# A graph network kernel: rankings, placing and unit records laid inside the counting of edges, and node layers handed from chunk to chunk

## The reference

```python
# stage 1: three graph-convolution layers 16 -> 64 -> 64 -> 16
deg = segment_sum(ones, col, N)              # with one loop per node added
norm = deg**-0.5 [row] * deg**-0.5 [col]
def gcn_layer(h, W, b):
    h = h @ W
    return segment_sum(norm[:, None] * h[row], col, N) + b
h = relu(gcn_layer(x, W1, b1)); h = relu(gcn_layer(h, W2, b2)); h = gcn_layer(h, W3, b3)
x = layernorm(x + h)
# stage 2: edge-conditioned attention, 16x16 channels per edge
w_m, w_a = edge_attr @ W_msg + b_msg, edge_attr @ W_attn + b_attn     # (E, 16, 16) each
e1, e2 = w_m * x[src][:, :, None], w_a * x[src][:, :, None]
attn = segment_softmax(e2, dst)
x = layernorm(x + segment_sum(e1 * attn, dst, N).sum(axis=1))
```

## Time and profile before

| what | us |
|---|---|
| median of three executions | 2631.48 (2610.61 to 2644.78) |
| span of the profiled execution, first to last instruction | 2618.5 |
| the median less the span | 13.0 |
| DVE busy | 1989.2 (76%) |
| PE busy | 1880.0 (72%) |
| ACT busy | 1458.7 (56%) |
| POOL busy | 1289.6 (49%) |

### The profile page before, as it was taken

The page is one execution under the profiler, slowest core; times in us unless marked ns, Lnnn a source line. Parts: engine busy times, 40 slices in busy tenths (PEclk is TensorE's granted clock), DMA queues, the critical chain, the costliest instruction groups (busy, mean ns, idle before and its releaser), DMA issues.

```text
span 2618.5 us, 37987 instructions
## 1 busy us (share of the span) xinstructions
PE 1880.0 (72%) x5814; PEld 706.3 (27%) x5815; DVE 1989.2 (76%) x3269; ACT 1458.7 (56%) x4999; POOL 1289.6 (49%) x1520
## 2 busy tenths in 40 slices
PE   2445676577982577787887777877888877888855
PEld 1111111132341133233333333333333333333322
DVE  5678999752011588888888888888898898988866
ACT  5124444210001576676777767777776776776643
POOL 2200000425556566656666657666666665666650
PEclk9789989788975699999999989999998998998877
DMA  2000000000001000000000000000000000000000
GB/s 31 17 23 4 0 0 0 2 10 17 11 13 15 9 10 10 9 10 9 10 9 10 9 10 9 10 9 10 9 10 9 10 10 9 9 10 9 9 5 7
DMA packets 85243, 25.74 MB, mean 10 GB/s; under 512 B 61677, under 2 KB 82271, under 8 KB 85087
## 3 DMA queue, kind: packets, MB, share of 16 engines
q0 software_dynamic: 36672, 18.09, 5.7%
q1 hardware_dynamic: 48463, 6.91, 1.8%
q10 hardware_dynamic: 80, 0.43, 0.1%
HBM read 22.73 MB, written 2.51 MB: 10 GB/s over the span
## 4 chain that ended last, share of the span: by engine, by line
issue 29%; DVE 25%; PE 23%; DVEq 17%; ACT 3%; POOL 1%; another core or an unknown queue 1%; DMA 1%; ACTq 0%; POOLq 0%; PEldq 0%; PEld 0%
PE pair L820 9%; DVE eo L1471 6%; DVE hot L1197 4%; DVEq L1490 4%; PE pw L711 3%; DVE eo L1514 2%; DVE eo L1505 2%; PE pw L807 2%; PE pw L708 2%; PE pw L707 2%; DVE top L1486 2%; ACT eo L1021 2%; DVE top L1491 2%; DVE bank L1499 2%; DVEq L1503 1%
## 5 line engine op out<-in xcount | busy, mean ns | idle before, releaser
L626 POOL DMA_INDIRECT nbr<-table,rec x928 | 961.0, 1036 | 527.3 <-ACT eo L1021 274.0
L820 PE MATMUL pair<-eo,ident 128*128 128x512 f32 x1856 | 890.0, 625 | 12.4 <-issue 7.7
L1021 ACT ACTIVATE eo<-pw,nbr 128x32 f32<-128x32 f32 x3712 | 694.3, 371 | 83.1 <-issue 66.9
L1471 DVE TENSOR_TENSOR eo<-pw,nbr 128x1024 f32 (+1 forms) x348 | 412.5, 1218 | 169.3 <-PE pw L807 94.4
L820 PEld LDWEIGHTS pair<-eo,ident 128*128 128x128 f32 x1856 | 366.2, 201 | 494.9 <-issue 479.6
L807 PE MATMUL pw<-wk,termsT 100*128 100x512 bf16 x928 | 307.5, 417 | 249.8 <-issue 173.8
L1197 DVE TENSOR_SCALAR hot<-iota_key,near_key 128x500 bf16<-128x500 f16 x974 | 273.8, 346 | 59.3 <-issue 31.9
L1010 ACT ACTIVATE eo<-eo 128x2048 f32<-128x2048 f32 x116 | 221.5, 1910 | 107.4 <-DVE eo L1505 85.1
L1514 DVE TENSOR_TENSOR eo<-eo x232 | 272.7, 1216 | 5.9 <-issue 4.0
L1505 DVE TENSOR_TENSOR eo<-eo,bank (+1 forms) x116 | 265.3, 2287 | 10.7
L672 PE MATMUL bank<-hot 128*128 128x500 bf16 x488 | 146.7, 414 | 145.4 <-DVE hot L1197 93.1
(11 more groups left out here) (245 smaller groups left out, 1815.6 us busy)
## 6 DMA issues: line engine op xcount, KB each, us to landing
nbr<-table,rec POOLq DMA_INDIRECT x928
rec<-unit_recs SPq DMA_DIRECT2D x116, 8.0 KB
attr<-in_edge_attr_dram,rec POOLq DMA_INDIRECT x116
unit_recs<-place SPq DMA_DIRECT2D x27, 64.0 KB
shared<-key_row SPq DMA_DIRECT2D x1, 1600.0 KB, 6.7
counts<-in_dst_dram SPq DMA_DIRECT2D x1, 448.0 KB
counts<-in_src_dram SPq DMA_DIRECT2D x1, 448.0 KB
place<-in_src_dram,at_i POOLq DMA_INDIRECT x26, 2.6
```

The costliest lines, as they stand in the source:

```text
L626: pool.indirect_dma_start(nbr[:, b, j * FEAT:(j + 1) * FEAT], None, table, bass.IndirectOffsetOnAxis(ap=rec[:, b, j:j + 1], axis=0)).then_ ...
L820: mm = pe.matmul(total, ident[:], eo[:, ring, j * 2 * CH:(j + 1) * 2 * CH], start=False, stop=(j == SLOT - 1), skip_group_check=True)
L1021: done = act.activation(eo[:, ring, lo:lo + wide], pw[:, j - 4, c * wide:(c + 1) * wide], ACT.Copy, scale=nbr[:, held, j * FEAT + c:j * FE ...
L1471: dve.tensor_tensor(eo[:, bass.ds(ring, 1), k * 4 * CH:(k + 1) * 4 * CH] .rearrange("p r (c f) -> p (r c) f", f=2 * FEAT), pw[:, 2 * (k % ...
```

## The change

- **Gathers** are issued two per pair of windows: POOL waits for DVE's window counter `s_near`, and for the gather four before, with four semaphores in place of one.
- **Counting below** is spread over pairs 5 to 17 on ACT, two tiles after each pair.
- **Ranks** begin four pairs later, at pair 22, one tile a pair; each tile is ranked in two halves of 1600 keys, one after each window. POOL adds the halves, makes the place and writes each tile's record at once.
- **Placing** (`place_nodes`, now only the copies) moves to DVE's pair 56 and the unit arithmetic (`unit_counts`) to pair 59, both within the counting.
- **The square roots** are written and laid over `y2T` by ACT's queue and no longer by SP's.
- **Layers:** with one plane PE no longer waits for `s_parts` in layers 1 and 2. It waits inside chunk 0 for each four tiles that DVE has split (`s_split`). The product with b2 stands behind `s_parts`. `plane_tables` is run in layers 1 and 2 only for several planes.

```diff
...
             for t in range(NT + 1):
                 to = dst_blk[:, t, :] if t < NT else dst_blk_last
+                if t % 2 == 0:
+                    pool.wait_ge(s_near, t + 5)
+                if t >= 4:
+                    pool.wait_ge(s_dblk[t % 4], 16 * (t // 4))
                 pool.indirect_dma_start(to, None, dst_blocks,
...
-            pool.wait_ge(s_rank, 1)
-            pool.tensor_scalar(rank_f, rank_f, NP - 1.0, 0.5, ALU.add, ALU.mult)
-            pool.drain()
-            pool.tensor_copy(rank_i, rank_f)
-            pool.drain()
             for t in range(NT):
+                here = slice(t, t + 1)
+                pool.wait_ge(s_rank, t + 1)
+                pool.tensor_tensor(rank_f[:, here], rank_f[:, here], rank_h[:, here], ALU.add)
+                pool.drain()
+                pool.tensor_scalar(rank_f[:, here], rank_f[:, here], NP - 1.0, 0.5, ALU.add, ALU.mult)
+                pool.drain()
+                pool.tensor_copy(rank_i[:, here], rank_f[:, here])
+                pool.drain()
                 pool.indirect_dma_start(rec_place, bass.IndirectOffsetOnAxis(ap=rank_i[:, t:t + 1], axis=0),
                                         rec_s[:, t, :], None).then_inc(s_recd, 16)
...
                 for a in range(NG):
+                    if layer and c == 0 and a % CT == 0:
+                        pe.wait_ge(s_split, splits + a // CT + 1)
+                        pe.sem_inc(s_settled_pe, 1)
                     cols = counts[:, a * DPAD + lo:a * DPAD + lo + n]
...
+            def count_below(t):
+
+                block_t = dst_blk[:, t, :] if t < NT else dst_blk_last
+                act.wait_ge(s_dblk[t % 4], 16 * (t // 4 + 1))
+                act.activation(signs[:, 0:P], block_t, ACT.Sign, bias=node_m[:, t:t + 1],
+                               scale=-1.0, accum_out=below[:, t:t + 1])
+                act.drain()
+
+            def rank_half(t, v):
+
+                part = slice(v * (NP // 2), (v + 1) * (NP // 2))
+                act.activation(signs[:, part], key_all[:, part], ACT.Sign, bias=key_neg[:, bass.ds(t, 1)],
+                               accum_out=(rank_f, rank_h)[v][:, bass.ds(t, 1)])
+                done = act.drain()
+                if v == 1:
+                    done.then_inc(s_rank, 1)
...
+            below_from = 5
+            rank_from = below_from + NT // 2 + 1 + 4
...
+                        keep_counts(0, below_from)
+                        for k in range(0, NT + 1, 2):
+                            keep_counts(below_from + k // 2, below_from + k // 2 + 1)
+                            with act.If(c < 1):
+                                for t in range(k, min(k + 2, NT + 1)):
+                                    count_below(t)
+                                if k + 2 > NT:
+                                    act.drain().then_inc(s_below, 1)
+                        keep_counts(below_from + NT // 2 + 1, rank_from)
                         with act.Fori(0, NT) as t:
...
+                            w = act.snap(wins, min_val=0, max_val=MANY)
+                            for v in range(2):
+                                keep_window(t + rank_from, w, v)
+                                with act.If(c < 1):
+                                    act.wait_ge(s_keyb, 16)
+                                    rank_half(t, v)
+                            act.reg_add(wins, wins, 1)
+                        keep_counts(rank_from + NT, NWIN // 2)
...
+            place_at = 56
...
-                    plane_tables()
                     if layer == 0:
-                        one_hot_plane()
+                        plane_tables()
+                        one_hot_head()
+                        one_hot_pairs(0, place_at)
                         with dve.If(c < 1):
-
-                            dve.wait_ge(s_rank, 1)
+                            place_nodes()
+                        one_hot_pairs(place_at, place_at + 3)
+                        with dve.If(c < 1):
+                            unit_counts()
+                        one_hot_pairs(place_at + 3, NWIN // 2)
+                        with dve.If(c < 1):
+
+                            dve.wait_ge(s_rank, NT)
...
                     dve.drain().then_inc(s_parts, 1)
-                    if layer == 0:
-                        with dve.If(c < 1):
-                            place_nodes()
+                    if layer == 1:
+                        with dve.If(p < 1):
+                            dve.wait_ge(s_sdb, 16)
+                            dve.wait_ge(s_sdc, 16)
+                            dve.tensor_scalar(y2T, y2T, b2c[:], None, ALU.mult)
+                            dve.drain()
...
```

More of the change, by code:

```diff
@@ L258, in gnn_kernel @@
         s_winr = sem("s_winr")
-        s_dblk = sem("s_dblk")
+        s_dblk = [sem(f"s_dblk{v}") for v in range(4)]
         s_below = sem("s_below")
@@ L422, in _ @@
             sp.dma_start(rec_p[:], rec_place.rearrange("(t p) c -> p t c", p=P)).then_inc(s_recp, 16)
[L424 to L428, removed]
             job = sp.alloc_register("sp_jobs")
@@ L696, in count_plane, with gather_chunk @@
                     pe.reg_add(wins, wins, 1)
-            def gather_chunk(layer, c, base):
+            def gather_chunk(layer, c, base, splits):
                 v = c % 2
@@ L746, in sum_sources @@
                 base = (c * ((NCH + 1) // 2), c * (NCH // 2))
+                splits = c * NCH if layer else None
                 for k in range(NCH + (2 if layer == 1 else 1)):
                     if k < NCH:
-                        gather_chunk(layer, k, base)
+                        gather_chunk(layer, k, base, splits)
                     if 1 <= k <= NCH:
@@ L764, in _, with counted @@
                     c = pe.snap(plane, min_val=0, max_val=MANY)
-                    pe.wait_ge(s_planes, c + 1)
-                    pe.sem_inc(s_settled_pe, 1)
+                    def counted():
+                        pe.wait_ge(s_planes, c + 1)
+                        pe.sem_inc(s_settled_pe, 1)
+                        count_plane()
+                        pe.wait_ge(s_parts, c + 1)
+                        pe.sem_inc(s_settled_pe, 1)
                     if layer == 0:
-                        count_plane()
+                        counted()
                     else:
                         with pe.If(np_ > 1):
-                            count_plane()
-                    pe.wait_ge(s_parts, c + 1)
-                    pe.sem_inc(s_settled_pe, 1)
+                            counted()
                     sum_sources(layer, c, pe.snap(mid, min_val=0, max_val=MANY))
@@ L892, in _, with keep_window @@
                 act.reg_mov(r, 0)
+            def keep_window(i, w, v):
+                act.wait_ge(s_full[v], w + 1)
+                act.copy(counts[:, 0:NG * DPAD].rearrange("p (a d) -> p a d", a=NG)
+                         [:, :, bass.ds(i * 2 * WIN + v * WIN, WIN)],
+                         bank[v][:, 0:NG * WIN].rearrange("p (a d) -> p a d", a=NG)
+                         ).then_inc(s_full_free[v], 1)
             def keep_counts(lo, hi):
@@ L898, in keep_counts @@
                     for v in range(2):
-                        act.wait_ge(s_full[v], w + 1)
-                        act.copy(counts[:, 0:NG * DPAD].rearrange("p (a d) -> p a d", a=NG)
-                                 [:, :, bass.ds(i * 2 * WIN + v * WIN, WIN)],
-                                 bank[v][:, 0:NG * WIN].rearrange("p (a d) -> p a d", a=NG)
-                                 ).then_inc(s_full_free[v], 1)
+                        keep_window(i, w, v)
                     act.reg_add(wins, wins, 1)
@@ L937, in _ @@
                 if layer == 1:
+                    act.wait_ge(s_sdd, 16)
+                    act.dma_start(y2T[:, 0:Y2A], row(sd_row[0:Y2A]).broadcast_to([HID, Y2A])).then_inc(s_sdb, 16)
                     act.wait_ge(s_y1, 1)
-                    act.wait_ge(s_sdd, 16)
                     act.dma_start(y2T[:, Y2A:NG * P], row(sd_row[Y2A:NG * P]).broadcast_to([HID, NG * P - Y2A])
@@ L1204, in one_hot_plane, with one_hot_pairs @@
                 dve.drain()
-                with dve.Fori(0, NWIN // 2) as i:
+            def one_hot_pairs(lo_pair, hi_pair):
+                with dve.Fori(lo_pair, hi_pair) as i:
                     w = dve.snap(windows, min_val=0, max_val=MANY)
@@ L1311, in place_nodes, with unit_counts @@
                 dve.drain().then_inc(s_place, 1)
+            def unit_counts():
                 dve.wait_ge(s_dmax, 1)
```

42 lines of the change are left out of this document (19 added, 23 removed).

## The result

| what | before | after |
|---|---|---|
| median of four executions, us | 2628.47 (2610.61 to 2644.78) | 2541.11 (2538.57 to 2550.02) |
| ratio, 95% interval | | 0.9686 [0.9636, 0.9736] |
| span of the profiled execution, us | 2618.5 | 2538.0 |

The spans differ by 80.5 us and the medians by 87.4, since the medians stand 10.0 and 3.1 us above the profiled spans. Little of that is time around a span: the profiled execution of the changed kernel took 2539.8 us, 1.8 above its own span, and every execution on record with both figures has between 1.7 and 2.8. What follows is about the 80.5. That difference is part of the finding. The chip of the first measurement is not on record.

The account below looks back on a forecast made before the run. DVE was taken to pace the counting, with only the 811 us before attention able to shrink. Gains 86.7 less costs 10.6 gave net 76.1: span 2542.4, plus 13.0, 2555 us; range of 8 in 10: 2536 to 2597.

Parts of the forecast that it names:

- the 13.0 us that I took as lying around the span: Whole execution: 13.0 us added to the forecast span of 2542.4 to give the forecast time of 2555.
- gathers: Counting, first burst: two gathers per pair of windows avoid DVE's slow windows; gain 22.5 us, bounds 0 to 24.9.
- keys: Counting: spread below-counts and four pairs before ranking cover the wait for keys; gain 22.3 us, bounds 15 to 22.3.
- ranks and price of places: Counting: ACT's half ranks pace part of 50 windows, cost 2 us; spread place writes still cost 1.8.
- placing and unit arithmetic: Counting: this work, formerly hidden behind PE's first chunk, now counts in full on DVE; cost 5.6 us, bounds 4 to 13.
- burst of places gone, rounds beside DVE: Late counting: 14.9 us excess of the place-write burst goes; unit-record rounds beside DVE's last 20 pairs cost 3.
- seams: PE's idle time ahead of layers 1 and 2, 19.0 and 6.45 us, goes; gain 25.5, bounds 18 to 28.
- start of attention: Before attention: early unit records let the table go out sooner; gain 3.3 us, bounds 1 to 4.
- the halting: Counting: DVE's own sequencer runs slow beside back-to-back indirect DMAs; excess 24.9 and 14.9 us in two bursts.
- my bound for new code to be fetched: Placing and unit arithmetic on DVE: cost up to 13 us if entering new code costs a fetch.
- Rival B: Counting: POOL's operations hold up DVE in full, 54 and 17 us; time 2623, no change; chance 0.12.
- rival A: Counting: DVE's slow sequencer is not cured by spreading; gains fall by 35.6 us, time 2591; chance 0.14.

Follow-up runs that it names:

- second chip: Kernel before and changed kernel, both unchanged, measured again later on another chip: changed kernel 2352.98 us, ratio 0.9816 to the kernel before.
- the run with one pair: Changed kernel with ACT's rankings starting one pair after the last below-count instead of four: 2361.76 us, ratio 0.9845 to the kernel before.
- the run with late records: Changed kernel with placing and unit arithmetic back behind the counting, in layer 0: 2373.97 us, ratio 0.9892 to the kernel before.
- The two runs above: Changed kernel with rankings one pair after the last below-count (2361.76 us), or with below-counts in a row and the four-pair gap kept (2365.43 us).

## Why the prediction was right

The time, 2541.1, lies in the range and 14 us below the 2555 forecast. The span was forecast at 2542.4 and is 2538.0, 4.4 us of the miss. The other 10 come from the 13.0 us that I took as lying around the span. No run shows that term: every execution on record with both figures has 1.7 to 2.8 us. I had set the median of three executions against the span of another, and these executions range over 34 us. In the terms of the forecast, from starts of windows and the rows above:

| term | forecast | first measurement | second chip |
|---|---|---|---|
| gathers: windows 1 to 41 | +22.5 | 133.6 - 110.3 = +23.3 | 116.7 - 110.2 = +6.5 |
| keys: 41 to 51 | +22.3 | 49.4 - 30.4 = +19.0 | 50.3 - 26.6 = +23.7 |
| ranks and price of places: 51 to 111 | -3.8 | 166.1 - 165.7 = +0.4 | 164.6 - 165.7 = -1.1 |
| placing and unit arithmetic: 111 to 121 | -5.6 | 28.4 - 33.1 = -4.7 | 29.5 - 33.1 = -3.6 |
| burst of places gone, rounds beside DVE: 121 to 159 | +11.9 | 118.1 - 108.7 = +9.4 | 106.6 - 108.8 = -2.2 |
| seams | +25.5 | 244.4 - 218.6 = +25.7 | 245.0 - 218.6 = +26.4 |
| start of attention | +3.3 | 16.4 - 12.8 = +3.6 | 14.2 - 12.7 = +1.4 |
| rest: head, end of counting, attention | 0 | 0.6 - 0.5 + 3.7 = +3.8 | 0.9 + 0.0 - 3.5 = -2.6 |
| sum | 76.1 | 80.5 | 48.6 |

(The second chip's sum is taken from unrounded terms.) The 6.5 us of the gathers on the second chip are not the halting: the granted clock of the kernel before was 0.82 from 44.7 to 90.4 us and 0.74 from 90.4 to 181 there, and spreading the gathers alone brought nothing. A term read from one pair of traces carries that much chance: windows 1 to 41, with the gathers spread, took 110.1 to 110.3 us in seven traces and 115.8 and 117.9 in two, where the granted clock was 0.85.

- *Keys.* 3.3 us under the forecast, and not for its reason: the stretch meets the dip of the clock at 158 to 180 us. On the second chip, with the clock at 0.92 there, the same ten windows give 23.7. My step, that the keys come some 14.5 us after the last below-count and four pairs cover it, is shown by the run with one pair.
- *Ranks.* ACT at 2.74 us a window was to pace 50 windows in part. The first thirty were 0.05 us longer each (2.80 against 2.75), the rest not; over the stretch nothing was lost. Within the bounds.
- *Placing and arithmetic.* 4.7, near the 5.6; my bound for new code to be fetched wasn't needed.
- *Rounds beside DVE.* I took 3 us; the run with late records puts it between 0.6 and 4.1. I had the rounds' pace wrong: 12.3 us each (380.5 to 491.4, nine rounds), not 9.4. POOL was held, not DVE. The multiplication L580 takes 382 ns in the median after 500 us, beside DVE's windows 566, and over 1 us in four of nine:

```profile
L580 POOL TENSOR_SCALAR place<-place x9: 452/566/1373, 390.0 to 483.2; 128x64 f32<-128x64 f32 x9
```

```profile
L580 POOL TENSOR_SCALAR place<-place x14: 382/382/1487, 512.5 to 634.1; 128x64 f32<-128x64 f32 x14
```

All of POOL's operations together take 0.52 us each from 382 to 491 us (65.03 us for 125) and 0.35 from 503 to 640 (68.96 for 196). DVE's hot rows keep their median of 344 ns both there and at 183 to 350 us. The page of the Trainium skill that the prediction weighed ("SBUF — State Buffer", Who interferes with whom) says whoever comes second blocks; the rows agree in that an operation is longer on one side, POOL's, beside a DVE busy 96% of the time. Which came first no row shows, and the price on DVE stayed at 4 us or less. Rival B needed DVE to be the loser, and falls. The slower rounds cost nothing, since the records were 72 us early.
- *Seams and the start of attention* came out within 0.3 us of their terms. POOL's last round begins at 648.5 us (forecast 638), attention's first gather at 734.20 (735). Attention itself is 3.7 us shorter in the first pair of traces and 3.5 longer in the second, at the same instructions; that is not the change's.

**The step that was right by its size and thin in its reason** is the first. I read the halting off two stretches of one trace, took the density of POOL's DMAs for its cause and gave the cure 36 of the 76 us. On that measurement each of the two terms came to within 3 us. That the density was the cause is not shown, and a measurement of the same kernels without the halting would have lacked both terms, so that this part of the number was right by luck as much as by reading. But in the runs on three chips later the same dense bursts halt nothing, and there the change is worth 45 us, which keys, seams and start of attention (23.7 + 26.4 + 1.4) less the costs make up. My rival A set out from "the cause is unknown"; what neither it nor the forecast had is that the effect may be absent and the kernel before 9% faster. What sets it, the chip, its state at the time or something else, stays open.

## What to carry to other kernels

A wait that an in-order engine makes for a long chain of others costs twice, once for the work it does in a block before the chain starts and once for the chain: cut the block into pieces between the units of its other duty, and leave a gap that covers the chain. The two runs above show that neither does it alone. Work for a later stage may be put beside the stage that paces even at a price (8.75 us here), if it otherwise ends last (21 us here net). And before a gap marked "issue" is made the reason for a change, look at the register instructions in the trace, and at the same kernel on a second chip: an effect read off one measurement may be that measurement's own.

## What the runs showed of the hardware

- Register instructions of DVE's sequencer, 40 to 60 ns in the median, take 0.7 us and a few of them 1.4 in one measurement, beside bursts of indirect DMAs and all through attention, which then takes 1807 us in place of 1616. Beside the first burst they start in steps of 0.70 or 1.40 us. No later run, on three chips, has one over 0.4 us on any engine, with the same bursts.
- A drain of POOL behind an indirect DMA and one small memset takes 1.34 us before the next operation starts; gather follows gather after 0.30.
- POOL's operations beside a DVE that is busy 96% take half as long again (0.52 us each and not 0.35), and DVE's loss is small: at most 4.1 us over nine rounds.
- The granted clock in one short stretch of the counting (158 to 180 us) was 0.61 in one measurement and 0.92 in another for the same kernel, and the ten windows around it took 30.4 and 26.6 us.
